# Six chunks of the expert stage started after 13 routed tiles instead of three after 22, with parts of the per-chunk work moved between engines

## The reference

```
xn = layernorm(x)
x = x + gnn(xn, src, dst) + linear_attention(xn)
t = layernorm(x)                      # 3125 tokens of 256
probs = softmax(t @ router_w.T)       # 8 experts
rw, re = top_k(probs, 2); rw /= rw.sum()
out = t
for e in range(8):
    h = gelu(t @ w1[e] + b1[e]); y = h @ w2[e] + b2[e]
    out += combine[:, e] * y          # each token has two experts
x = x + out
```

## Time and profile before

| | us |
|---|---|
| median of three runs | 431.22 (428.87 to 433.67) |
| the profiled execution | 430.48, of which the span is 428.8 |
| TensorE busy | 404.5 (94% of the span), x3141 |
| VectorE busy | 311.2 (73%) |
| ScalarE busy | 265.8 (62%) |
| GpSimd busy | 183.5 (43%) |
| first layer L1681 / second layer L1692, busy | 65.6 / 64.0 |
| indirect sends L634, L653, L660, busy | 24.7 / 31.0 / 30.6 |
| mean granted TensorE clock | 0.962 |

### The profile page before, as it was taken

How to read it: one execution, slowest core, us unless ns; L and a number is a source line. 1 busy time by engine, 2 the same in 40 slices (tenths; PEclk the granted TensorE clock), 3 DMA queues, 4 the chain that set the end, 5 groups by cost and what they waited for, 6 DMA issues and landing times.

```text
span 428.8 us, 10052 instructions
## 1 busy us (share of the span) xinstructions
PE 404.5 (94%) x3141; PEld 318.8 (74%) x3141; DVE 311.2 (73%) x785; ACT 265.8 (62%) x676; POOL 183.5 (43%) x298
## 2 busy tenths in 40 slices
PE   4989899997999999999999999978999999999995
PEld 1767678776677777777755667854999998988894
DVE  3688858967899999999727653667688887655553
ACT  1756655575788888888824614441776766666663
POOL 4058969246100010001091114464456565655655
PEclk9899999999999999999999987577999999999999
DMA  8927310006589999999997961124465665467651
GB/s 211 194 70 255 90 26 8 1 2 125 106 152 172 172 175 167 179 184 189 167 215 227 308 224 63 65 81 120 151 190 188 187 210 159 140 202 207 186 177 38
DMA packets 111827, 64.11 MB, mean 150 GB/s; under 512 B 87985, under 2 KB 102202, under 8 KB 111646
## 3 DMA queue, kind: packets, MB, share of 16 engines
q1 hardware_dynamic: 104590, 48.14, 51.0%
q0 software_dynamic: 6368, 14.47, 9.6%
q10 hardware_dynamic: 816, 0.85, 0.8%
HBM read 24.00 MB, written 21.44 MB: 106 GB/s over the span
## 4 chain that ended last, share of the span: by engine, by line
PE 52%; POOL 12%; issue 11%; DMA 10%; DVE 10%; ACT 3%; SPq 1%; POOLq 0%; DVEq 0%
PE bank L1432 9%; PE bank L1381 8%; PE bank L1475 6%; POOL xs_next L653 5%; PE bank L1346 4%; PE bank L1444 4%; DMA region_a<-xs_next 4%; PE bank L1355 3%; POOL out L660 3%; DMA out<-region_a 3%; PE bank L1612 2%; PE bank L1594 2%; PE bank L1454 2%; DMA xs_next<-region_a 2%; POOL region_a L648 2%
## 5 line engine op out<-in xcount | busy, mean ns | idle before, releaser
L725 ACT CAST region_a<-bank 128x500 bf16<-128x500 f32 (+1 forms) x119 | 70.0, 673 | 14.8 <-PE bank L1381 14.8
L1681 PE MATMUL bank<-region_a,region_c 128*128 128x128 f32 x496 | 65.6, 275 | 0.0
L1692 PE MATMUL bank<-region_c,region_a 128*128 128x256 f32 x248 | 64.0, 380 | 0.0
L1681 PEld LDWEIGHTS bank<-region_a,region_c 128*128 128x128 f32 x496 | 60.3, 191 | 0.1
L1142 DVE COPY region_c<-region_w 128x1026 f32 x62 | 43.5, 701 | 19.2 <-issue 17.7
L605 POOL COPY wide<-den 125x256 f32<-125x256 f32 x25 | 13.0, 518 | 100.6 <-DVE den L1057 100.6
L1381 PE MATMUL bank<-region_a 128*128 128x125 bf16 x625 | 52.9, 219 | 1.5 <-ACT region_a L725 1.4
L1381 PEld LDWEIGHTS bank<-region_a 128*128 128x128 bf16 x625 | 42.2, 101 | 13.6 <-ACT region_a L725 3.2
L989 DVE TENSOR_TENSOR region_a<-iota,keys 128x3150 bf16<-128x3150 bf16 x25 | 44.9, 1796 | 5.4 <-PE bank L1381 5.4
L1304 DVE SCALAR_TENSOR_TENSOR region_a<-bank,region_a 128x256 f32<-128x256 f32 x62 | 30.0, 484 | 22.1 <-PE bank L1692 19.9
L815 ACT COPY region_a<-bank 128x256 f32<-128x256 f32 x62 | 23.1, 373 | 36.9 <-PE bank L1670 36.8
(11 more groups left out here) (239 smaller groups left out, 775.6 us busy)
## 6 DMA issues: line engine op xcount, KB each, us to landing
region_a<-xs_next SPq DMA_DIRECT2D x31, 259.0 KB, 2.9
region_w<-in_w SPq DMA_DIRECT2D x4, 1024.0 KB, 9.7
region_a<-xs SPq DMA_DIRECT2D x31, 131.0 KB, 2.4
rows<-in_x SPq DMA_DIRECT2D x5, 560.0 KB
xs_next<-null SPq DMA_DIRECT2D x8, 259.0 KB, 4.9
xs_next<-null SPq DMA_DIRECT2D x1, 1554.0 KB, 11.4
xs<-null SPq DMA_DIRECT2D x8, 131.0 KB, 3.1
region_q<-in_b SPq DMA_DIRECT2D x1, 1024.0 KB, 9.6
```

What stands on the lines that cost most here:

```text
L725: nc.scalar.copy(to, count_bank(n)[:, 0:w * TP].rearrange("p (c t u) -> p c t u", c=w, t=NT)).then_inc(adj_done, 1)
L1681: last = nc.tensor.matmul(hid_ps[c % 2][:, f * P:(f + 1) * P], wc[:, c % 3, k * D + f * P:k * D + (f + 1) * P], xT[:, c % 2, k * P:(k + 1) ...
L1692: last = nc.tensor.matmul(y_ps[c % 2][:, 0:D], hT[:, c % 2, f * P:(f + 1) * P], wc[:, c % 3, (2 + f) * D:(3 + f) * D], start=False, stop=( ...
```

## The change

`SURE_G` = 2: the sure chunks are now found from the counts after 13 tiles, and `SURE` becomes 6. `whole_chunks` computes how many full chunks each expert's list holds by then, and `sure_chunks` lists the first six of them over all experts. They are loaded when 13 tiles are sent. VectorE reads four experts' registers and copies two experts' weights after `weigh(4)`, a third before `weigh(5)`; later registers are read one chunk ahead. TensorE drops the 26 dummy matmuls, starts chunk 0 after `logits(5)`, and runs `positions(5)` after the first `first_layer`. The first table is made after the first steps of chunk 0 and 3, the second table in seven parts behind chunks 8 to 14; SyncE waits for it before chunk 31. From chunk 6 on, GpSimd makes the row weights (`row_weights`); for odd chunks ScalarE restores the residual (`restore`). `xch` moves into another region, and the odd chunks' results into the bank `spare`.

```diff
-SURE = -(-ROUT[-1][0] * TP // (NX - 1)) // P
+SURE_G = 2
+SECOND = 8
+SURE_T = ROUT[SURE_G][1]
+SURE = -(-(SURE_T * TP - (NX - 1) * (P - 1)) // P)
 CAP = 27 * TP
 FRONT = 2 * TP
 NULLS = MC - -(-N // P)
...
-        xt_ps, hid_ps, y_ps = (y0, y1), (m0, m1), (h0, h1)
+        xt_ps, hid_ps, y_ps = (y0, y1), (m0, m1), (h0, spare)
...
+        xch = r.take(P, XB * WIDE).rearrange("p (s d) -> p s d", s=XB)
...
             sp.wait_ge(sure_known, 1)
             sp.wait_ge(nulls_stored, (2 + 2 * NX) * 16)
-            sp.wait_ge(sent, ROUT[-1][0] * 16)
+            sp.wait_ge(sent, SURE_T * 16)
             for c in range(SURE):
                 load_chunk(c)
             sp.wait_ge(table_done, 1)
-            sp.wait_ge(sent_last, (NT - ROUT[-1][0]) * 16)
-            for c in range(SURE, NCH):
+            sp.wait_ge(sent_last, (NT - SURE_T) * 16)
+            for c in range(SURE, MC):
+                load_chunk(c)
+            sp.wait_ge(table_done, 2)
+            for c in range(MC, NCH):
                 load_chunk(c)
...
@@ block.gpsimd @@
-                                             rows[:, t, :], None).then_inc(sent if t < ROUT[-1][0] else sent_last, 16)
+                                             rows[:, t, :], None).then_inc(sent if t < SURE_T else sent_last, 16)
...
+            def row_weights(c):
+                pool.wait_ge(turned_gap, c + 1)
+                nc.gpsimd.tensor_scalar(xch[:, c % XB, W_LOW:W_HIGH + 1], halves[:], turn[:, c:c + 1], 0.5, ALU.mult,
+                                        ALU.add).then_inc(weights_made, 1)
...
                 if c + 1 < MC:
                     goals(c + 1)
+                    if c + 1 >= SURE:
+                        row_weights(c + 1)
                 hand_on(c)
...
@@ block.scalar @@
-                if c == 1:
-                    act.wait_ge(table_done, 1)
...
+            def restore(c):
+                s = c % XB
+                nc.scalar.activation(xch[:, s, PART:WIDE], xch[:, s, 0:D], ACT.Identity,
+                                     scale=xch[:, s, SPAN:SPAN + 1], bias=xch[:, s, MEAN:MEAN + 1]).then_inc(restored, 1)
...
                     turn_gap(c)
+                    if c % 2 == 1:
+                        restore(c)
...
@@ block.vector @@
+            def whole_chunks():
+                now = pos_from(SURE_T, SURE_T + 1)[0:1, 0:NX]
+                dve.wait_ge(pos_ready, SURE_G + 1)
+                chain(nc.vector.scalar_tensor_tensor(whole[:, 0, :], now, 1.0 / P, base_p[:], ALU.mult, ALU.subtract))
+                chain(nc.vector.tensor_scalar(whole[:, 0, :], whole[:, 0, :], MAGIC, -MAGIC, ALU.add, ALU.add))
...
             def sure_chunks():
...
+                chain(nc.vector.tensor_tensor(whole_upto[:], up_to[:], whole[:].to_broadcast([1, NX, NX]), ALU.mult))
+                nc.vector.tensor_scalar(skipped[:, 0, :], whole[:, 0, :], -float(P), float(CAP), ALU.mult, ALU.add)
+                chain(nc.vector.tensor_reduce(whole_ends[:, 0, :], whole_upto[:], AX_X, ALU.add))
+                chain(nc.vector.tensor_tensor(
+                    sure_past[:], whole_ends[:].to_broadcast([1, SURE, NX]),
+                    chunk_of[:, 0:SURE].rearrange("p (c a) -> p c a", a=1).to_broadcast([1, SURE, NX]), ALU.is_le))
+                chain(nc.vector.tensor_tensor(sure_skip[:], sure_past[:], skipped[:].to_broadcast([1, SURE, NX]),
+                                              ALU.mult))
+                nc.vector.tensor_reduce(sure_at[:, 0, :], sure_past[:], AX_X, ALU.add)
+                chain(nc.vector.tensor_reduce(sure_at[:, 1, :], sure_skip[:], AX_X, ALU.add))
+                nc.vector.tensor_tensor(row_of[:, 0:SURE], sure_at[:, 1, :], sure_row[:], ALU.add)
+                nc.vector.tensor_copy(expert_i[:, 0:SURE], sure_at[:, 0, :]).then_inc(sure_known, 1)
+                chain(nc.vector.tensor_scalar(sure_end[:, 1:NX + 1], whole_ends[:, 0, :], float(SURE), float(P), ALU.min,
+                                              ALU.mult))
+                nc.vector.tensor_tensor(taken[:], sure_end[:, 1:NX + 1], sure_end[:, 0:NX], ALU.subtract)
...
+            nc.vector.tensor_scalar(base_p[:], base[0:1, 0:NX], 1.0 / P, 0.5 - 0.25 / P, ALU.mult, ALU.add)
+            nc.vector.tensor_scalar(up_to[:], e_diff[:], 0.0, None, ALU.is_ge)
+            nc.vector.memset(sure_end[:, 0:1], 0.0)
...
                 choose(g)
+                if g == SURE_G + 1:
+                    sure_chunks()
                 if g + 2 < NR:
                     add_graph(g + 2)
+                if g == NR - 1:
+                    copy_weights(2, experts[2])
                 weigh(g)
+                if g == SURE_G:
+                    whole_chunks()
                 if g == NR - 2:
-                    sure_chunks()
...
+                    dve.wait_ge(w_in, 80)
+                    experts = [expert_of(c) for c in range(4)]
+                    copy_weights(0, experts[0])
+                    copy_weights(1, experts[1])
 
...
             def weigh_rows(c):
...
+                    if c % 2 == 0:
+                        link(nc.vector.tensor_scalar(xch[:, s, PART:WIDE], xch[:, s, 0:D], xch[:, s, SPAN:SPAN + 1],
+                                                     xch[:, s, MEAN:MEAN + 1], ALU.mult, ALU.add))
+                    else:
+                        dve.wait_ge(restored, c // 2 + 1)
+                    if c >= SURE:
+                        dve.wait_ge(weights_made, c - SURE + 1)
+                    else:
+                        dve.wait_ge(turned_gap, c + 1)
+                        link(nc.vector.scalar_tensor_tensor(xch[:, s, W_LOW:W_HIGH + 1], halves[:], turn[:, c:c + 1],
+                                                            half[:], ALU.mult, ALU.add))
...
+            def chunks_of(r2):
...
+            def second_table(part):
+                if part == 0:
+                    chunks_of(1)
...
+            chunks_of(0)
+            ends_of(0)
+            dve.wait_ge(xch_in[0], 16)
+            weigh_rows(0)
+            copy_weights(3, experts[3])
+            lists_passed(0)
+            row_steps(0)
+            first_rows(0)
+            dve.wait_ge(table_done, 1)
+
+            e = expert_of(4)
+            for c in range(1, NCH):
+                if 1 < c < NCH - 2:
+                    copy_weights(c + 2, e)
+                    if c == MC - 3:
+                        dve.wait_ge(table_done, 2)
+                    if c + 3 < NCH:
+                        e = expert_of(c + 3)
...
                 dve.wait_ge(xch_in[c % XB], (c // XB + 1) * 16)
                 weigh_rows(c)
+                second_table(c - SECOND)
...
@@ block.tensor @@
                     transpose_tokens(g + 1, 0)
                 if g + 2 < NR:
                     graph3(g + 2)
-                positions(g)
                 if g + 1 < NR:
+                    positions(g)
                     keep_clock(spare, 3)
                     logits(g + 1)
 
@@ -1694,15 +1776,11 @@
                                             skip_group_check=True)
                 last.then_inc(y_ready, 1)
 
-            pe.wait_ge(tkT_done, copies_to(NR))
-            keep_clock(m0, 12)
-            pe.wait_ge(pos_read, NR)
             pe.wait_ge(x2_done, NT)
-            pe.wait_ge(sent, ROUT[-1][0] * 16)
-            keep_clock(m0, 14)
             turn_rows(0)
             turn_rows(1)
             first_layer(0)
+            positions(NR - 1)
             for c in range(NCH):
                 if c + 2 < NCH:
                     turn_rows(c + 2)
```

More of the change, by code:

```diff
@@ L1136, in chain, with expert_of, copy_weights @@
                 link(ins)
[L1138 to L1139 removed]
+            def expert_of(c):
+                return dve.value_load(expert_i[0:1, c:c + 1], min_val=0, max_val=NX - 1)
+            def copy_weights(c, e):
                 if c >= 3:
@@ L1260, in _ @@
-            chain(nc.vector.tensor_scalar(nch[:], nch[:], MAGIC, -MAGIC, ALU.add, ALU.add))
-            for r2 in range(2):
-                last = nc.vector.tensor_tensor(upto[:, r2, :, :], up_to[:], nch[:, r2:r2 + 1, :].to_broadcast([1, NX, NX]),
-                                               ALU.mult)
-            chain(last)
-            chain(nc.vector.tensor_reduce(ends[:], upto[:], AX_X, ALU.add))
-            for r2 in range(2):
-                last = nc.vector.tensor_tensor(past[:, r2, :, :], ends[:, r2:r2 + 1, :].to_broadcast([1, MC, NX]),
-                                               chunk_of[:].rearrange("p (c a) -> p c a", a=1).to_broadcast([1, MC, NX]),
-                                               ALU.is_le)
@@ L1270, in _ @@
-            chain(last)
-            nc.vector.tensor_tensor(passed_by, past[:, 1, :, :], ends[:, 0:1, :].to_broadcast([1, MC, NX]), ALU.mult)
-            chain(nc.vector.tensor_reduce(expert_f[:], past[:], AX_X, ALU.add))
-            chain(nc.vector.tensor_reduce(need[:], passed_by, AX_X, ALU.max))
```

(36 more changed lines are left out.)

91 lines of the change are left out of this document (41 added, 50 removed).

## The result

The changed kernel takes 425.23 us (median of 4 runs, 423.80 to 426.81); the kernel before, run beside it, 430.38. The ratio is 0.9882 [0.9841, 0.9922]: 5.1 us less, and the forecast was 425.5. Of the profiled executions, the span went from 428.8 to 425.1 us, 3.7 less. The median's difference was 5.1 us in the first comparison and 2.9 in the second, so the gain is some 3 to 5 us.

What follows compares the result with a forecast made beforehand. TensorE was taken to bound the expert stage at 1.98 us per chunk, after a hole waiting for GpSimd's sends. 6.7 less 1.0, 0.5, 0 and 0.2 gave 5.0 us: 430.5 to 425.5 us, range 422.5 to 430.0.

Steps and rivals of the forecast that it cites:

- The gate: Start of expert stage: chunk 6 instead of chunk 3 waits for the last send; at most 6.7 us to be had.
- The delay of that send: GpSimd's last send comes later through small VectorE instructions and weight copies: 1.0 us lost, between 0 and 2.
- TensorE and VectorE in time: Before chunk 6: TensorE's four iterations done by 297.9, first table between 296 and 298.5; 0.5 us lost, between 0 and 2.5.
- The tie: Before chunk 6: first table ends between 296 and 298.5, sends seen at about 298; 0.5 us subtracted.
- VectorE as the new bound at the start: Rival: at the start the table comes 2.5 us late and chunks 4 and 5 wait for weights; 428 us, chance 0.15.
- Per chunk: Expert loop: relief of VectorE saves nothing, second table's 3.4 us fits in free time; 0 us lost, between 0 and 1.
- GpSimd: Expert loop: row weights before hand-overs delay these 0.2 to 0.8 us; 0.2 us lost in all, between 0 and 1.5.
- the third rival: GpSimd sets the pace in first-table chunks once cast and row weights cost over 0.8 us together; 435.5 us, chance 0.10.
- ScalarE's tables: Rival: tables reload around the odd chunks' residual, two loads of 1.28 us each time; 450 us or more, chance 0.02.

Runs made afterwards that it cites:

- e1: Changed kernel, but the six sure chunks wait for 22 sent tiles and the last positions precede chunk 0 on TensorE: 436.21 us.
- e5: The changed kernel timed again, unedited, in the second comparison: 426.20 us, ratio 0.9913 to the kernel before.
- e6: Changed kernel with chunk 1's row weighting and chunk 4's weight copy ahead of the first table's rest on VectorE: 428.47 us.
- e2: Kernel before plus only registers read one chunk ahead, odd residuals on ScalarE and row weights on GpSimd from chunk 6: 430.02 us, ratio 0.9986.
- e9: Changed kernel with each expert's register read on VectorE right before its weight copy, ahead of the loop and in it: 430.97 us.
- after: The changed kernel itself, as first measured against the kernel before: 425.23 us, ratio 0.9882.
- e3: Changed kernel with all residuals and row weights back on VectorE, registers still read ahead: 429.93 us, ratio 0.9996.
- e12: Changed kernel with GpSimd's row weights computed twice, first into a spare tile: 430.54 us, ratio 0.9980.
- e7: Changed kernel with the weight copies of chunks 0 and 1 on ScalarE, two registers read on VectorE ahead of the loop: 426.55 us.
- e8: Changed kernel with chunk 4's copy early, chunks 0 and 1's copies on ScalarE, second table's parts behind every second chunk 8 to 20: 426.45 us.

## Why the prediction was right, and where it was not

1. *The gate* (chunk 6 and not chunk 3 waits for the last send): right. e1 takes it back, and no gain is left.
2. *The delay of that send*, 1.0 us: it was 1.86. But 0.92 of that is there at 226 us, in code that the change does not touch (the same TensorE step starts at 226.94 instead of 226.02). The change's own part is 0.94, of which 0.46 are sends beside weight copies and about 0.15 the three small instructions; the rest is there by the 13th send and was not followed further. In e5, where that TensorE step starts at 226.03, the last send is 0.97 us late, so the size of this step was right. Another term was not: chunk 6's load landed after 2.2 us, where I had 2.80 (step 1). In the first profile the two errors nearly cancel: the load landed at 302.1, where steps 1 and 2 give 300.92 + 1.0 = 301.9. That is luck.
3. *TensorE and VectorE in time*, chunk 6 at 301 to 303: it was 302.18. TensorE by itself would have come there 1.75 us earlier, at 300.43; the 297.9 in the prediction is four iterations at 1.98 us each, and the granted clock was at 0.50 until 293 and at 1.00 from 294 on. The tie named there was real, and e5 and e6 show three gates in it, not two: the last send, the first table, and the weight copy of chunk 4, which the prediction had only in a rival (VectorE as the new bound at the start).
4. *Per chunk, 0, between 0 and 1*: this step failed. Chunks 12 to 20 lost 2.35 us to the second table. Its parts are 4.6 us of VectorE (the sum of their 18 instructions from 312.83 to 327.76), where I had 3.4, and I paid them from the mean free time of a chunk. A late result on VectorE was passed on through ScalarE within the same chunk (0.94 us of waiting there, then 0.64 on TensorE, at 319.31). Moreover "saves nothing" holds only without the second table (e2). Beside it, registers read ahead are worth 3.7 us between chunks 12 and 20 (e9 against after), the two moves 1.5 (e3). Without the one or the other the median stood at that of the kernel before.
5. *GpSimd*, 0.2: no loss is seen, and TensorE's waits for loads in the second table stayed at 1.6 us. But casts rose from 202 to 441 ns and the row weights take 353 ns, 0.79 together, where the third rival set its limit at 0.8; e12 shows that another 0.40 us per chunk is too much.

Followed chunk by chunk, the lead is 5.40 us at chunk 6 (forecast 5.2), 3.06 at chunk 20 after step 4's loss, and 3.68 at chunk 61, as chunks 20 to 61 took 0.6 us less than before (forecast 0.2 more, in the second table); the idle time that the profile lists before loads there fell only from 1.7 to 1.6 us, so what gave the 0.6 stays open. The trace gives 3.7 us where the sum was 5.0; the medians gave 5.1 and 2.9. So 425.5 was right within what can be measured, with an error of some 2 us in step 4 that the medians do not resolve, and partly by the luck named in step 2.

Of the rivals, ScalarE's tables were not reloaded: its only load after 280 us is one of 1.28 us ahead of the loop.

## What to carry to other kernels

Work taken off an engine that had free time was worth nothing here (ratio 0.9986, e2) until something else was put in its place; test the relief together with what it makes room for (e2 against e3 and e9). When a wait is taken away, list everything that releases the next step: here three gates lay within 1 us, and moving one only moved the wait (e6, e7). A mean of free time was no cover for work that stood in front of a result someone waited for (2.35 us lost from chunk 12 to 20, step 4).

## What was not expected of the hardware

- A read of a register cost VectorE more than the two instructions suggest: they take 0.30 and 0.18 us, yet four reads in a row left VectorE idle for 2.71 us (after), 2.47 (e5) and 2.74 (e6), 0.62 to 0.69 each (the prediction took 0.6). A read that ran beside a copy was nearly hidden: in e9 the read ahead of the first copy left VectorE idle for 0.59 us, the next one, beside that copy, for 0.06.
- Some of GpSimd's indirect sends were slower beside VectorE's weight copies (1.42 and 1.33 us, the 19th and the 21st of the changed kernel), but not all: the 24th took 0.97 us although a whole copy (294.92 to 295.61) ran beside it, and in e5 the 19th (from 287.12) took 0.97 although two copies (from 287.24, 1.35 us) ran beside it. None was slower beside the same copies on ScalarE (0.97, e7). What decides between the two was not tested.
- A copy of 128x1026 took ScalarE about 1.0 us (1.98 us for two) and VectorE 0.69.
- One idle stretch of 2.62 us (e6) and one of 2.96 (e8) were followed by the half clock (0.50), those of 1.75 (after) and 2.20 (e9) were not (1.00). Length alone does not sort them: in e8 an idle stretch of 1.27 us, ended at 287.47, was followed by 0.50 as well. No rule is drawn from five cases.
